# Routing flags laid out with pairs of token blocks innermost

## The chip, the cores and the metric

The kernel runs on one core of a Trainium2 chip. The metric is the device time of one execution in microseconds. The kernel before takes 2205.02 us (median of 3 runs, 2200.27 to 2205.75). The profiled execution took 2211.22 us; its traced span is 2209.5 us.

## The reference, cut to what matters

```python
x = x + xattn(layernorm(x), ctx, ...)        # x: 8 x 512 x 512; 16 heads, 1601 keys
xf = layernorm(x).reshape(-1, 512)           # 4096 tokens
logits = xf @ w_gate                         # 8 experts
top_logits, top_idx = top_k(logits, 2)
weights = softmax(top_logits)
# every token goes through its two experts (512 -> 256 gated -> 512),
# the results are weighted, added, and added to x
```

The kernel does not sort the tokens. It gives each of the 8192 (token, choice) pairs a slot: 72 tiles of 128 lanes, where each tile belongs to one expert. For each slot it needs a list entry: which token sits there, with what weight, and in which slot the token's other choice sits. The change is in the making of that list.

## The kernel before, in words

The program has phases, with a barrier of all engines between them (`phase`, line 35). Attention takes the first 1735 us or so of the span. Then `route` (line 1378) makes the slot list, and `run_experts` (line 1645) gathers the token rows by that list and runs the 72 tiles through the experts.

In `route` the 4096 tokens lie as 128 partitions by TT = 32 blocks. Each choice c (0 or 1) of a token has a tile number (`where`) and a lane in it (`within`). The list is made by matmuls with one-hot flags (lines 1485 to 1490): for each c and each block n, a 128x128 matrix `lane_hot[c][:, :, n]` (token by lane) is the stationary operand, and a 128x432 matrix `marks[c][:, :, :, n]` (token by 6 values x 72 tiles) is the moving one. All 64 products are added up in one bank, `ps_table`, which then holds for each lane and tile the 6 values: row, block, weight high, weight low, other tile, other lane.

Before the change both flag arrays have the block index innermost: `lane_hot` is [128 lanes][32 blocks] and `marks` is [6 values][72 tiles][32 blocks] of 2-byte numbers in each partition. A matmul takes one n, so it reads every 32nd number, one each 64 bytes, in both operands.

VectorE fills them. Its program in this part is: `lane_hot` for both c by a comparison of a constant array `lane` with the broadcast `within` (line 1590); the flags `tile_hot` in the same way from `number` and `where` (line 1592); then for each c five products of 128x2304 (lines 1598 to 1605), of which the last is written over `tile_hot` itself and waits for ScalarE's product of the sixth value (line 1475). TensorE's 32 products for c = 0 wait for `marked[0]`, those for c = 1 for `marked[1]`. The constants `lane` and `number` are made by ScalarE at the start of the phase (lines 1468 and 1469) as full 128x4096 and 128x2304 arrays, which lie in space borrowed from `marks[1]`.

The same phase loads and splits the experts' weights, 8 experts in 3 pieces each. For each piece: a DMA to `e_raw` (waits for the VectorE split of the same piece of the expert before), ScalarE's high part (line 1465), VectorE's low part (`low_pieces`, line 1502). The low parts are written out by hand between VectorE's routing steps. The last before the list are `low_pieces(3)` at line 1614; then VectorE waits for `listed` (line 1616), reads the bank and works out `slots`, `partners`, `targets` (lines 1617 to 1633), and does the three low parts that remain (line 1634). That ends the phase.

Of the kernel before, what the change touches and what calls it, by code (L numbers as in the profile page):

```python
# [7 lines left out]
F16 = mybir.dt.float16  # L8
# [3 lines left out]
ALU = mybir.AluOpType  # L12
ACT = mybir.ActivationFunctionType
AX = mybir.AxisListType

P = 128
# [3 lines left out]
E, TOPK, FF = 8, 2, 256  # L20
# [42 lines left out]
def sbuf(nc, held, name, shape, dt):  # L63
    return held.enter_context(nc.sbuf_tensor(name, shape, dt))


def banks(nc, held, names, dt=F32):
    n = 512 if dt == F32 else 1024
    return [held.enter_context(nc.psum_tensor(x, [P, n], dt)) for x in names]
# [137 lines left out]
TT = B * N // P  # L207
TILES = 72
# [1164 lines left out]
VALUES = 6  # L1373
# [4 lines left out]
def route(nc, k, t):  # L1378

    with ExitStack() as held, phase(nc) as (block, sem):  # L1380
# [5 lines left out]
        def weight_piece(e, n, part):  # L1386
            return t["wi"][:, e, part, 2 * n:2 * n + 2, :] if n < 2 else t["wo"][:, e, part, :, :]

        sb = lambda name, shape, dt=F32: sbuf(nc, held, "r_" + name, shape, dt)
# [9 lines left out]
        pos, where_f, where, within_f, within = (  # L1399
            sb("pos", [P, TOPK, TT]), sb("where_f", [P, TOPK, TT]), sb("where", [P, TOPK, TT], F16),  # L1400
            sb("within_f", [P, TOPK, TT]), sb("within", [P, TOPK, TT], F16))
        w_high = sb("w_high", [P, TOPK, TT], F16)
        w_low = sb("w_low", [P, TOPK, TT], F16)
        block_i, block_f = sb("block_i", [P, TT], I32), sb("block_f", [P, TT], F16)
        row_i, row_1 = sb("row_i", [P, 1], I32), sb("row_1", [P, 1])
        spare = sb("spare", [P, 1])
        lane_i, number_i = sb("lane_i", [P, P, 1], I32), sb("number_i", [P, TILES, 1], I32)
        lane_hot = [sb(f"lane_hot{c}", [P, P, TT], F16) for c in range(TOPK)]
        marks = [sb(f"marks{c}", [P, VALUES, TILES, TT], F16) for c in range(TOPK)]
        tile_hot = [marks[c][:, VALUES - 1, :, :] for c in range(TOPK)]  # L1410
        number = marks[1][:, 2, :, :]
        lane = marks[1][:, 0:2, :, :].rearrange("p v q n -> p (v q n)")[:, 0:P * TT].rearrange("p (l n) -> p l n", n=TT)
        second, tile_1, other_tile, other_lane = (
            sb("second", [P, TOPK, TT]), sb("tile_1", [P, TOPK, TT]), sb("other_tile", [P, TOPK, TT], F16),
            sb("other_lane", [P, TOPK, TT], F16))
# [12 lines left out]
        ps_before, ps_total, ps_table = banks(nc, held, ["r_pb", "r_pt", "r_ps"])  # L1428
        made, spread, step, hot_ready, summed, gap_ready, ratio_ready, tile_ready, listed = (
            sem("r_" + n) for n in ("made", "spread", "step", "hot_ready", "summed", "gap_ready", "ratio_ready",  # L1430
                                    "tile_ready", "listed"))
        marked = [sem(f"r_marked{c}") for c in range(TOPK)]

        @block.gpsimd
        def _(pool):
            pool.iota(experts_i[:, :], [[1, E]], base=0, channel_multiplier=0)
            pool.iota(tile_i[:, :], [[1, TILES]], base=0, channel_multiplier=0)
            pool.iota(lane_i[:, :, :], [[1, P]], base=0, channel_multiplier=0)
            pool.iota(number_i[:, :, :], [[1, TILES]], base=0, channel_multiplier=0)
            pool.iota(block_i[:, :], [[1, TT]], base=0, channel_multiplier=0)  # L1440
            pool.iota(row_i[:, :], [[1, 1]], base=1, channel_multiplier=1)
            pool.affine_select(out=before[:, :], in_=k["ones"][:, :], compare_op=ALU.is_gt, fill=0.0, base=0,
                               pattern=[[1, P]], channel_multiplier=-1).then_inc(made, 1)
# [15 lines left out]
        @block.scalar  # L1459
        def _(act):  # L1460
            def high_pieces(experts):
                for e in experts:
                    for n in range(PIECES):
                        act.wait_ge(loaded[n], 32 * (e + 1))
                        act.mul(weight_piece(e, n, 0), raw[n][:, :, :], WSCALE).then_inc(high, 1)

            act.wait_ge(made, 1)
            act.copy(lane, lane_i[:, :, :].to_broadcast([P, P, TT]))
            act.copy(number, number_i[:, :, :].to_broadcast([P, TILES, TT])).then_inc(spread, 1)
            act.wait_ge(gap_ready, 1)  # L1470
            act.activation(ratio[:, :], gap[:, :], ACT.Exp, scale=1.0 / WSCALE).then_inc(ratio_ready, 1)
            high_pieces(range(0, 4))
            for c in range(TOPK):
                act.wait_ge(tile_ready, TOPK)
                act.activation(marks[c][:, 0, :, :], tile_hot[c], ACT.Identity,
                               scale=row_1[:, 0:1]).then_inc(marked[c], 1)
                high_pieces(range(4 + 2 * c, 6 + 2 * c))

        @block.tensor
        def _(pe):  # L1480
            pe.wait_ge(hot_ready, 1)
            flat = any_hot_b[:, :, :].rearrange("p t e -> p (t e)")
            pe.matmul(ps_before[:, 0:TT * E], before_b[:, :], flat, start=True, stop=True)
            pe.matmul(ps_total[:, 0:TT * E], ones_b[:, :], flat, start=True, stop=True).then_inc(summed, 1)
            for c in range(TOPK):
                pe.wait_ge(marked[c], 2)
                for n in range(TT):
                    last = pe.matmul(ps_table[:, 0:VALUES * TILES], lane_hot[c][:, :, n],
                                     marks[c][:, :, :, n].rearrange("p v q -> p (v q)"),
                                     start=(c == 0 and n == 0), stop=(c == TOPK - 1 and n == TT - 1))  # L1490
            last.then_inc(listed, 1)

        @block.vector
        def _(dve):
# [3 lines left out]
            def low_pieces(count):  # L1498
                flat = lambda a: a.rearrange("p a b -> p (a b)")
                for e, n in itertools.islice(pieces, count):  # L1500
                    dve.wait_ge(high, PIECES * e + n + 1)
                    dve.scalar_tensor_tensor(out=flat(weight_piece(e, n, 1)), in0=flat(raw[n][:, :, :]),
                                             scalar=WSCALE, in1=flat(weight_piece(e, n, 0)), op0=ALU.mult,
                                             op1=ALU.subtract).then_inc(split, 1)

            for n in range(TT):
                last = dve.max(best[:, n, :], t["logits"][:, n, :])
            done(last)
            for n in range(TT):
                last = dve.max_index(index[:, n, :], best[:, n, :], t["logits"][:, n, :])  # L1510
# [8 lines left out]
            for c in range(TOPK):  # L1519
                last = dve.tensor_tensor(hot[:, c, :, :], experts[:, None, :].to_broadcast([P, TT, E]),  # L1520
                                         chosen[:, c, :, None].to_broadcast([P, TT, E]), ALU.is_equal)
# [33 lines left out]
            for c in range(TOPK):  # L1555
                last = dve.tensor_tensor(hot[:, c, :, :], hot[:, c, :, :], place[:, :, :], ALU.mult)
# [26 lines left out]
            for c in range(TOPK):  # L1583
                dve.tensor_tensor(other_tile[:, c, :], tile_1[:, 1 - c, :], second[:, c, :], ALU.mult)
                last = dve.tensor_tensor(other_lane[:, c, :], within_f[:, 1 - c, :], second[:, c, :], ALU.mult)
            done(last)

            dve.wait_ge(spread, 1)
            for c in range(TOPK):
                dve.tensor_tensor(lane_hot[c][:, :, :], lane, within[:, c, None, :].to_broadcast([P, P, TT]), ALU.is_equal)  # L1590
            for c in range(TOPK):
                dve.tensor_tensor(tile_hot[c], number, where[:, c, None, :].to_broadcast([P, TILES, TT]),
                                  ALU.is_equal).then_inc(tile_ready, 1)
            dve.wait_ge(tile_ready, TOPK)
            low_pieces(1)
            for c in range(TOPK):
                over = lambda a: a[:, c, None, :].to_broadcast([P, TILES, TT])
                dve.tensor_tensor(marks[c][:, 1, :, :], tile_hot[c],
                                  block_f[:, None, :].to_broadcast([P, TILES, TT]), ALU.mult)
                dve.tensor_tensor(marks[c][:, 2, :, :], tile_hot[c], over(w_high), ALU.mult)  # L1600
                low_pieces(2)
                dve.tensor_tensor(marks[c][:, 3, :, :], tile_hot[c], over(w_low), ALU.mult)
                dve.tensor_tensor(marks[c][:, 4, :, :], tile_hot[c], over(other_tile), ALU.mult)
                dve.wait_ge(marked[c], 1)
                dve.tensor_tensor(tile_hot[c], tile_hot[c], over(other_lane), ALU.mult).then_inc(marked[c], 1)
                low_pieces(2)


# [238 lines left out]
def program(nc, x, ctx_t, wq, bq, wkv_t, bkv, wp, bp, w_gate, wi_0, wi_1, w_out, out):  # L1847
# [14 lines left out]
    with ExitStack() as held:  # L1862
# [52 lines left out]
        t["slots"], t["partners"], t["targets"] = (sb(n, [P, TILES], U32) for n in ("slots", "partners", "targets"))  # L1915
        t["slot_weight"] = sb("slot_weight", [P, TILES])
        route(nc, k, t)
        run_experts(nc, k, t)

# [22 lines left out]
```

## Time and profile before

| | |
|---|---|
| median of 3 runs | 2205.02 us |
| profiled execution, time | 2211.22 us |
| its span | 2209.5 us |
| TensorE busy | 84% of the span |
| VectorE busy | 81% |
| ScalarE busy | 61% |
| GpSimd busy | 44% |

The shares are means over phases with different limits. The routing phase is some 110 us of the span, and it is read by its own timeline: for each engine, when an instruction starts, how long it takes, and what ended the idle time before it. PEclk is the clock that TensorE was granted, as a share of 2.4 GHz; 0.50 is 1.2 GHz.

### The profile page before, as it was taken

How to read it: one execution, taken by the hardware profiler on the slowest of the kernel's cores; microseconds unless marked ns; L12 is line 12 of the kernel's file. 1: busy time of each engine (PE TensorE's matmuls, PEld its weight loads, DVE VectorE, ACT ScalarE, POOL GpSimd, SP SyncE). 2: the span in 40 equal slices, each digit the busy share in tenths (PEclk: the TensorE clock that was granted, in tenths of full speed). 3: DMA queues.
4: the chain of work that ended last, by engine and by line, in shares of the span. 5: the costliest groups of instructions: out<-in, count | busy, mean ns of one | idle time of the engine just before them, and what ended most of it. 6: DMA issues, size and time to landing. Idle time of an engine off the chain costs nothing. (4 is left out here: it accounts for less than half of the span.)

```text
span 2209.5 us, 60580 instructions
## 1 busy us (share of the span) xinstructions
PE 1849.1 (84%) x24745; PEld 1264.9 (57%) x24804; DVE 1795.7 (81%) x2402; ACT 1351.7 (61%) x1944; POOL 969.0 (44%) x900
## 2 busy tenths in 40 slices
PE   1379998999988989998989898989986147999996
PEld 1247676666666666666666666667763012555553
DVE  4469999899998998998999999988996582666665
ACT  0347877777777777777777787777766431233222
POOL 0011653383265336434723553373435101677675
PEclk9889999999999999999999999999998556999998
DMA  2322332233233223323322331331221351566785
GB/s 86 99 80 56 96 93 53 78 103 85 59 99 101 61 74 100 95 56 87 108 79 62 105 105 44 88 108 56 65 54 49 99 159 62 176 200 218 242 264 176
DMA packets 152822, 225.40 MB, mean 102 GB/s; under 512 B 33860, under 2 KB 87108, under 8 KB 152544
## 3 DMA queue, kind: packets, MB, share of 16 engines
q1 hardware_dynamic: 130736, 166.89, 26.2%
q0 software_dynamic: 21808, 54.58, 8.0%
q8 instruction: 202, 3.31, 0.7%
q14 instruction: 76, 0.62, 0.1%
HBM read 131.37 MB, written 71.32 MB: 92 GB/s over the span
## 5 line engine op out<-in xcount | busy, mean ns | idle before, releaser
L764 DVE TENSOR_TENSOR a_p_low<-a_p 128x1024 f16<-128x1024 f32 (+1 forms) x896 | 1095.5, 1245 | 141.5 <-ACT a_p L642 133.6
L642 ACT ACTIVATE a_p<-ps_s 128x1024 f32<-128x1024 f32 (+1 forms) x896 | 862.6, 967 | 390.4 <-PE ps_s L493 382.1
L493 PE MATMUL ps_s<-a_q_stack,a_k_stack 96*128 96x512 f16 (+1 forms) x1664 | 516.0, 385 | 81.1 <-DMA a_k_stack<-a_k_parts 55.0
L604 PE MATMUL ps_o<-a_v,a_p 128*128 128x65 f16 (+1 forms) x6656 | 448.3, 195 | 19.3 <-ACT a_o_sums L668 8.9
L604 PE MATMUL ps_o<-a_v,a_p_low 128*128 128x65 f16 (+1 forms) x6656 | 448.0, 194 | 0.0
L526 PEld LDWEIGHTS ps_p<-wkv,a_ctx 128*128 128x128 f16 x4992 | 329.6, 99 | 166.1 <-DVE a_v L779 59.0
L526 PE MATMUL ps_p<-wkv,a_ctx 128*128 128x128 f16 x4992 | 378.7, 221 | 44.4 <-DVE a_v L779 44.1
L604 PEld LDWEIGHTS ps_o<-a_v,a_p 128*128 128x128 bf16 (+1 forms) x6656 | 352.7, 99 | 101.2 <-DVE a_p_low L764 26.9
L510 PE MATMUL ps_p<-a_ctx,wkv 128*128 128x384 f16 (+2 forms) x1536 | 347.6, 336 | 36.9 <-DVE a_ctx L402 34.2
L604 PEld LDWEIGHTS ps_o<-a_v,a_p_low 128*128 128x128 f16 (+1 forms) x6656 | 318.4, 98 | 0.0
L510 PEld LDWEIGHTS ps_p<-a_ctx,wkv 128*128 128x128 f16 x1536 | 147.7, 98 | 184.6 <-DVE a_ctx L402 30.9
L905 POOL TENSOR_TENSOR a_o_full<-a_o_sums 128x128 f32<-128x128 f32 x128 | 133.4, 1071 | 214.9 <-ACT a_o_sums L668 214.9
L402 POOL TENSOR_TENSOR a_ctx<-a_ctx_raw,a_ctx 128x384 f16<-128x384 f32 (+2 forms) x112 | 169.0, 1521 | 116.1 <-ACT a_ctx L678 115.2
L1735 PE MATMUL f_ph<-wi_parts,f_xt 128*128 x864 | 200.8, 383 | 2.6 <-DVE f_xt L1802 2.6
L909 POOL TENSOR_TENSOR a_o_full<-a_o_full,o_inv 128x128 f32<-128x128 f32 x128 | 142.0, 1138 | 84.8 <-DVE o_inv L786 84.1
L493 PEld LDWEIGHTS ps_s<-a_q_stack,a_k_stack 96*128 96x128 f16 (+1 forms) x1664 | 114.4, 100 | 87.2 <-issue 81.7
L1676 POOL DMA_INDIRECT f_xs<-d_xr,slots x72 | 82.2, 1142 | 181.2 <-POOLq L48 109.4
L956 POOL TENSOR_TENSOR a_o_full<-a_o_full,a_x_in 128x512 f32<-128x512 f32 x32 | 87.7, 2741 | 153.7 <-DVE a_o_full L865 153.7
L1735 PEld LDWEIGHTS f_ph<-wi_parts,f_xt 128*128 128x128 f16 x864 | 84.8, 98 | 106.0 <-issue 6.0
L1788 ACT ACTIVATE f_gate<-f_ph 128x256 f32<-128x256 f32 x72 | 27.7, 385 | 142.6 <-PE f_ph L1735 142.6
L950 POOL TENSOR_TENSOR a_x_in<-a_x_in,bp_row 128x512 f32<-128x512 f32 x32 | 55.3, 1730 | 125.5 <-DMA a_x_in<-in_x_dram 125.4
L936 POOL TENSOR_SCALAR a_q_nmean<-a_q_mv 128x4 f32<-128x4 f32 x8 | 5.7, 719 | 234.3 <-DVE a_q_rstd L791 234.3
(232 smaller groups left out, 2211.9 us busy)
## 6 DMA issues: line engine op xcount, KB each, us to landing
a_k_stack<-a_k_parts SPq DMA_DIRECT2D x384, 80.0 KB, 2.1
d_ys<-f_y SPq DMA_DIRECT2D x72, 256.0 KB
a_ctx_raw<-in_ctx_dram SPq DMA_DIRECT2D x64, 192.0 KB, 2.5
a_q_stack<-d_q_t SPq DMA_DIRECT2D x96, 128.0 KB, 3.6
a_xm<-in_x_dram SPq DMA_DIRECT2D x8, 1024.0 KB, 5.9
a_ctx_raw<-in_ctx_dram SPq DMA_DIRECT2D x32, 256.0 KB, 4.6
d_q_t<-a_q_parts SPq DMA_DIRECT2D x32, 256.0 KB, 2.7
d_q_full<-a_xm SPq DMA_DIRECT2D x32, 256.0 KB, 2.9
```

The lines of the kernel that those rows point to most:

```text
L402: eng.tensor_tensor(t["ctx"][:, 1, c, a:e], t["ctx_raw"][p % NRAW][:, 0:e - a], t["ctx"][:, 0, c, a:e], ALU.subtract).then_inc(ctx_split, 1)
L493: mm = pe.matmul(t["ps_s"][s % 2][0:r, n * N:(n + 1) * N], t["k_stack"][v % 2][0:TERMS * DH, j, kt * P:kt * P + r], t["q_stack"][v % 2][0: ...
L510: mm = pe.matmul(bank(job)[:, 0:e - a], t["wkv"][:, w_part, c, c0:c0 + P], t["ctx"][:, x_part, c, a:e], start=(m == 0), stop=(m == TERMS * ...
L526: mm = pe.matmul(bank(job)[:, n * P:(n + 1) * P], t["ctx"][:, x_part, c, kt * P:(kt + 1) * P], t["wkv"][:, w_part, c, c0:c0 + P], start=(m ...
L604: mm = pe.matmul(t["ps_o"][:, q * VC:(q + 1) * VC], part[0:r, n * N + q * P:n * N + (q + 1) * P], val, start=(g == 0 and n == 0 and low == ...
L642: act.activation(t["p"][s % NP][0:r, 0:len(tiles) * N], t["ps_s"][s % 2][0:r, 0:len(tiles) * N], ACT.Exp, scale=float(DH) ** -0.5 / WSCALE ...
L764: dve.tensor_tensor(t["p_low"][s % NP][0:r, 0:n], full, high, ALU.subtract).then_inc(lows, 1)
L905: last = pool.tensor_tensor(heads[:, j], sums[:, j, :, 0:DH], sums[:, j, :, DH:2 * DH], ALU.add)
L909: last = pool.tensor_tensor(heads[:, j], heads[:, j], t["o_inv"][:, v, j, :, None].to_broadcast([P, QT, DH]), ALU.mult)
L956: pool.tensor_tensor(t["o_full"][b % 2][:, m, :], t["o_full"][b % 2][:, m, :], t["x_in"][i % 2][:, :], ALU.add).then_inc(x2_ready, 1)
L1676: pool.indirect_dma_start(out=xs[n % NX][:, :], out_offset=None, in_=t["xr"][:, :], in_offset=bass.IndirectOffsetOnAxis(ap=t["slots"][:, n ...
L1735: last = pe.matmul(ps_h[n % 2][:, :], xt[n % 2][:, x_part, c, :], t["wi"][:, bass.ds(e, 1), w_part, c, :].rearrange("p a f -> p (a f)"), s ...
```

## The change

The block index n is split into n // 2 and n % 2. The arrays become `lane_hot` [16][128 lanes][2] and `marks` [16][6 values][72 tiles][2]. A matmul for one n now reads every second number, one each 4 bytes, in both operands, in a run of 128 or 432. The matmuls are the same in number, order and shape. `lane` and `number` become small arrays of their own (128x2 and 72x2 numbers), read again for each of the 16 outer steps. VectorE's twelve products and comparisons of 2304 elements and two of 4096 keep their element counts; the per-token operand is now read as a pair that is repeated for all lanes or tiles (`over`), where before a run of 32 was repeated.

No instruction moves. In ScalarE's program, at the start of the routing phase, the two casts that make the constants become smaller:

```order
 L1459 UNCONDITIONAL_BRANCH
 L1468 ACT_TABLE_LOAD
-L1468 CAST r_marks<-r_lane_i 128x4096
-L1469 CAST r_marks<-r_number_i 128x2304
+L1468 CAST r_lane<-r_lane_i 128x256
+L1469 CAST r_number<-r_number_i 128x144
 L1471 ACTIVATE r_ratio<-r_gap 128x32
 L1465 ACTIVATE wi_parts<-e_raw 128x1024 x2
```

Nothing else stands there than before; the shapes are what changed.

```diff
-        lane_hot = [sb(f"lane_hot{c}", [P, P, TT], F16) for c in range(TOPK)]
-        marks = [sb(f"marks{c}", [P, VALUES, TILES, TT], F16) for c in range(TOPK)]
-        tile_hot = [marks[c][:, VALUES - 1, :, :] for c in range(TOPK)]
-        number = marks[1][:, 2, :, :]
-        lane = marks[1][:, 0:2, :, :].rearrange("p v q n -> p (v q n)")[:, 0:P * TT].rearrange("p (l n) -> p l n", n=TT)
+        lane, number = sb("lane", [P, P, 2], F16), sb("number", [P, TILES, 2], F16)
+        lane_hot = [sb(f"lane_hot{c}", [P, TT // 2, P, 2], F16) for c in range(TOPK)]
+        marks = [sb(f"marks{c}", [P, TT // 2, VALUES, TILES, 2], F16) for c in range(TOPK)]
+        mark = lambda c, v: marks[c][:, :, v, :, :]
+        tile_hot = [mark(c, VALUES - 1) for c in range(TOPK)]
...
-            act.copy(lane, lane_i[:, :, :].to_broadcast([P, P, TT]))
-            act.copy(number, number_i[:, :, :].to_broadcast([P, TILES, TT])).then_inc(spread, 1)
+            act.copy(lane[:, :, :], lane_i[:, :, :].to_broadcast([P, P, 2]))
+            act.copy(number[:, :, :], number_i[:, :, :].to_broadcast([P, TILES, 2])).then_inc(spread, 1)
...
-                    last = pe.matmul(ps_table[:, 0:VALUES * TILES], lane_hot[c][:, :, n],
-                                     marks[c][:, :, :, n].rearrange("p v q -> p (v q)"),
+                    last = pe.matmul(ps_table[:, 0:VALUES * TILES], lane_hot[c][:, n // 2, :, n % 2],
+                                     marks[c][:, n // 2, :, :, n % 2].rearrange("p v q -> p (v q)"),
...
+            def over(a, count):
+                return a.rearrange("p (h two) -> p h two", two=2)[:, :, None, :].to_broadcast([P, TT // 2, count, 2])
+
+            def along(a, count):
+                return a[:, None, :, :].to_broadcast([P, TT // 2, count, 2])
+
             dve.wait_ge(spread, 1)
             for c in range(TOPK):
-                dve.tensor_tensor(lane_hot[c][:, :, :], lane, within[:, c, None, :].to_broadcast([P, P, TT]), ALU.is_equal)
+                dve.tensor_tensor(lane_hot[c][:, :, :, :], along(lane, P), over(within[:, c, :], P), ALU.is_equal)
...
-                dve.tensor_tensor(marks[c][:, 2, :, :], tile_hot[c], over(w_high), ALU.mult)
+                dve.tensor_tensor(mark(c, 2), tile_hot[c], over(w_high[:, c, :], TILES), ALU.mult)
...
```

The other products of `marks` and ScalarE's (line 1475) are rewritten in the same way as the last pair of lines.

## Rows read from the trace of the kernel before

**Rows 1.** The page: span, and the granted TensorE clock in 40 slices (tenths).
```profile
span 2209.5 us, 60580 instructions
...
PEclk9889999999999999999999999999998556999998
```

**Rows 2.** Waits, 1735 to 1870 us: total us, times, longest us.
```profile
POOL f_xs L1676 <- POOLq L48: 109.4, 1, 109.4
...
DVE r_table L1617 <- PE r_ps L1488: 24.2, 1, 24.2
...
DVE r_marks L1605 <- ACT r_marks L1475: 2.9, 1, 2.9
```

**Rows 3.** Line 1488's instructions: ns min/median/max, first and last start.
```profile
L1488 PEld LDWEIGHTS r_ps<-r_marks,r_lane_hot x64: 141/148/162, 1795.7 to 1841.3; 128*128 128x128 f16 x64
L1488 PE MATMUL r_ps<-r_marks,r_lane_hot x64: 900/916/939, 1795.7 to 1842.1; 128*128 128x432 f16 x64
```

**Rows 4.** Windows: length, busy us (count) of PE, PEld, DVE, ACT, POOL; PEclk, DMA.
```profile
1795.60:1843.00 47.40, 47.29 (x64) 9.41 (x64) 18.62 (x19) 12.59 (x11) 0.00 (x0) 0.50 0.34 101
```

**Rows 5.** Timeline of TensorE: start us, us, line, operation, [idle before, releaser].
```profile
1795.68 47.29 PE L1488 MATMUL r_ps<-r_marks,r_lane_hot 128*128 128x432 f16 x64 [39.45 <-DVE r_marks L1605]
1856.82 1.03 PE L1724 MATMUL f_px<-id,f_xs 128*128 128x128 f16 x8 [13.85 <-DMA f_xs<-d_xr,slots]
1858.73 5.30 PE L1735 MATMUL f_ph<-wi_parts,f_xt 128*128 x12 [0.88 <-DVE f_xt L1802]
...
1865.40 2.76 PE L1735 MATMUL f_ph<-wi_parts,f_xt 128*128 x12 [0.87 <-DVE f_xt L1802]
```

**Rows 6.** Windows at the start of the experts: the granted clock rises.
```profile
1863.00:1864.00 1.00, 1.00 (x5) 0.45 (x4) 0.00 (x0) 0.00 (x0) 0.00 (x0) 0.50 0.57 234
1864.00:1865.00 1.00, 0.53 (x9) 0.36 (x6) 0.43 (x1) 0.38 (x1) 0.00 (x0) 0.99 0.02 8
```

**Rows 7.** Timeline of VectorE, around its wait for the list.
```profile
1808.13 1.36 DVE L1605 TENSOR_TENSOR r_marks<-r_marks,r_other_lane 128x2304 f16<-128x2304 f16 x1 [2.89 <-ACT r_marks L1475]
...
1817.53 1.22 DVE L1502 SCALAR_TENSOR_TENSOR wo_parts<-e_raw,wo_parts 128x1024 f16<-128x1024 f32 x1 [1.14 <-ACT wo_parts L1465]
1843.00 0.61 DVE L1617 COPY r_table<-r_ps 128x432 f32<-128x432 f32 x1 [24.25 <-PE r_ps L1488]
...
1846.08 2.36 DVE L1502 SCALAR_TENSOR_TENSOR wi_parts<-e_raw,wi_parts 128x1024 f16<-128x1024 f32 x2
1848.36 1.22 DVE L1502 SCALAR_TENSOR_TENSOR wo_parts<-e_raw,wo_parts 128x1024 f16<-128x1024 f32 x1
```

**Rows 8.** Timeline of ScalarE: constants, exponential, and the last expert's high parts.
```profile
1742.73 3.60 ACT L1468 CAST r_marks<-r_lane_i 128x4096 f16<-128x4096 int32 x1
...
1753.50 0.23 ACT L1471 ACTIVATE r_ratio<-r_gap 128x32 f32<-128x32 f32 x1 [5.16 <-DVE r_gap L1512]
...
1818.83 1.06 ACT L1465 ACTIVATE wi_parts<-e_raw 128x1024 f16<-128x1024 f32 x1 [1.33 <-DMA e_raw<-in_L_ffn_wi_dram]
1821.30 1.06 ACT L1465 ACTIVATE wi_parts<-e_raw 128x1024 f16<-128x1024 f32 x1 [1.42 <-DMA e_raw<-in_L_ffn_wi_dram]
1823.09 1.06 ACT L1465 ACTIVATE wo_parts<-e_raw 128x1024 f16<-128x1024 f32 x1 [0.73 <-DMA e_raw<-in_L_ffn_wo_dram]
```

**Rows 9.** Groups of VectorE instructions by shape: count | busy us, mean ns | idle.
```profile
L1590 DVE TENSOR_TENSOR r_lane_hot<-r_marks,r_within 128x4096 f16<-128x4096 f16 x2 | 4.5, 2288 | 0.0
...
L1598 DVE TENSOR_TENSOR r_marks<-r_marks,r_block_f 128x2304 f16<-128x2304 f16 x2 | 2.7, 1352 | 0.0
...
L1520 DVE TENSOR_TENSOR r_hot<-r_experts,r_chosen 128x256 f32<-128x256 f32 x2 | 0.8, 422 | 0.0
...
L1609 DVE TENSOR_TENSOR r_passed<-r_tile_f,r_starts 1x576 f32<-1x576 f32 x1 | 0.7, 740 | 0.0
...
L1523 DVE TENSOR_TENSOR r_any_hot<-r_hot 128x256 f32<-128x256 f32 x1 | 0.4, 425 | 0.0
```

**Rows 10.** Timeline of GpSimd: its first gather for the experts.
```profile
1851.97 1.19 POOL L1676 DMA_INDIRECT f_xs<-d_xr,slots  x1 [109.42 <-POOLq L48]
```

More of the change, by code:

```diff
@@ L1474, in _ @@
                 act.wait_ge(tile_ready, TOPK)
-                act.activation(marks[c][:, 0, :, :], tile_hot[c], ACT.Identity,
+                act.activation(mark(c, 0), tile_hot[c], ACT.Identity,
                                scale=row_1[:, 0:1]).then_inc(marked[c], 1)
@@ L1586, in _ @@
             done(last)
+            def over(a, count):
+                return a.rearrange("p (h two) -> p h two", two=2)[:, :, None, :].to_broadcast([P, TT // 2, count, 2])
+            def along(a, count):
+                return a[:, None, :, :].to_broadcast([P, TT // 2, count, 2])
             dve.wait_ge(spread, 1)
             for c in range(TOPK):
-                dve.tensor_tensor(lane_hot[c][:, :, :], lane, within[:, c, None, :].to_broadcast([P, P, TT]), ALU.is_equal)
+                dve.tensor_tensor(lane_hot[c][:, :, :, :], along(lane, P), over(within[:, c, :], P), ALU.is_equal)
             for c in range(TOPK):
-                dve.tensor_tensor(tile_hot[c], number, where[:, c, None, :].to_broadcast([P, TILES, TT]),
+                dve.tensor_tensor(tile_hot[c], along(number, TILES), over(where[:, c, :], TILES),
                                   ALU.is_equal).then_inc(tile_ready, 1)
@@ L1596, in _ @@
             for c in range(TOPK):
-                over = lambda a: a[:, c, None, :].to_broadcast([P, TILES, TT])
-                dve.tensor_tensor(marks[c][:, 1, :, :], tile_hot[c],
-                                  block_f[:, None, :].to_broadcast([P, TILES, TT]), ALU.mult)
-                dve.tensor_tensor(marks[c][:, 2, :, :], tile_hot[c], over(w_high), ALU.mult)
+                dve.tensor_tensor(mark(c, 1), tile_hot[c], over(block_f[:, :], TILES), ALU.mult)
+                dve.tensor_tensor(mark(c, 2), tile_hot[c], over(w_high[:, c, :], TILES), ALU.mult)
                 low_pieces(2)
-                dve.tensor_tensor(marks[c][:, 3, :, :], tile_hot[c], over(w_low), ALU.mult)
-                dve.tensor_tensor(marks[c][:, 4, :, :], tile_hot[c], over(other_tile), ALU.mult)
+                dve.tensor_tensor(mark(c, 3), tile_hot[c], over(w_low[:, c, :], TILES), ALU.mult)
+                dve.tensor_tensor(mark(c, 4), tile_hot[c], over(other_tile[:, c, :], TILES), ALU.mult)
                 dve.wait_ge(marked[c], 1)
-                dve.tensor_tensor(tile_hot[c], tile_hot[c], over(other_lane), ALU.mult).then_inc(marked[c], 1)
+                dve.tensor_tensor(tile_hot[c], tile_hot[c], over(other_lane[:, c, :], TILES),
+                                  ALU.mult).then_inc(marked[c], 1)
                 low_pieces(2)
```

## The prediction, made before the changed kernel ran

> **What bounds the kernel now.** I read the page first. TensorE's clock is at 0.9 or more in most of the 40 slices and dips to 0.5 in two of them after slice 30 [rows 1]; slices are 55 us long, so these two lie about the routing phase, between attention and experts. The shares of busy time say nothing there. The waits of that stretch come next. The longest is GpSimd's, 109.4 us until the barrier [rows 2]: the experts start when the routing phase ends, with nothing of the experts beside it. So what the routing phase loses or gains at its end goes into the span one to one, and the question is what ends that phase.
>
> VectorE ends it: its last instruction is the third of the last low parts, from 1848.36 to 1849.58 [rows 7]. Before these it worked off the list, from 1843.00 to 1846.08, and before the list it stood idle for 24.25 us until TensorE had finished line 1488 [rows 2, 7]. TensorE runs its 64 products without a pause from 1795.68 to 1842.97 [rows 5], though it had to wait for nothing: the marks of the second choice were ready when VectorE's last product ended at 1808.13 + 1.36 = 1809.49 [rows 7]. So between 1818.75 (VectorE's last low part before the wait ends, 1817.53 + 1.22) and 1843.00 the phase is bound by the rate of TensorE alone, and the reader should ask what that rate is.
>
> It is 47.29 us / 64 = 0.739 us for one product of 432 columns, or 1.71 ns per column. The granted clock is 0.50 all through, 1.2 GHz [rows 4]. At that same clock the experts' first 12 products of 512 columns took 5.30 us [rows 5, 6], 0.442 us each, 0.863 ns per column. They read their operands in one run; line 1488 reads a number each 64 bytes. The flag products thus take twice as long per column as dense ones at an equal clock. The record of 916 ns for one matmul [rows 3] is longer than the 739 from start to start, since they overlap; I use starts.
>
> **The change part by part.** *Moving operand.* Now a number each 4 bytes. I take the dense rate: 432 x 0.863 = 0.373 us per product at 1.2 GHz. At 2.4 GHz the experts' next 12 took 2.76 us, 0.230 us each for 512 columns, so 0.194 us for 432 [rows 5, 6]. The ends for the unknown stride of 4 bytes are the dense rate and today's 0.739 us (no gain at all); 4 bytes is nearest to the dense rows of 2-byte steps, so I take these. *Stationary operand.* 148 ns per load now [rows 3]; between nothing and 148 ns shows: if the load were not hidden behind the product before, a product would take 0.373 + 0.148 = 0.52 us. In the dense rows a load stands for each product as well, and 0.442 us for 512 columns leaves 0.015 us for it over 512 / 1.2 GHz = 0.427, so I take it as hidden.
>
> *The first 32 products* start at 1795.7 as before and need at most 32 x 0.373 = 11.9 us, to 1807.6. That is before 1809.49, so they no longer queue in front of the second 32. *The second 32* start at 1809.5 and take 32 x 0.194 = 6.2 us if the clock is up, 32 x 0.373 = 11.9 us if it isn't: end at 1815.7 to 1821.4. Which one is open: the clock rose in the experts within 7.1 us of TensorE's first work (1856.82 to about 1863.9 [rows 5, 6]), while in 47 us of line 1488 it never did [rows 4]. With dense reads I would expect it to rise in the first batch; whether it survives the pause of some 2 to 4 us before the second I can't tell.
>
> *VectorE until the list.* Two comparisons of 4096 elements at 2.288 us and twelve of 2304 at 1.352 us [rows 9]. From these two, 1792 elements are 0.936 us, 0.522 ns per element or 1.04 ns per pair: the numbers are taken in pairs. After the change outputs are still dense runs (144 or 4096 numbers), the first input too, and the second is one pair read again and again. I take no change. The ends are below nothing only by noise, since the element rate can't rise, and above by the unpaired rate (the first rival below). The row nearest to a repeated word is line 1520, where the second input repeats one 4-byte number 8 times: 422 ns for 256, against 425 with plain operands [rows 9]. So re-reading a word costs nothing there.
>
> *ScalarE.* The cast of 3.60 us [rows 8] and its smaller neighbour shrink to a small part. ScalarE then waits 5.16 us for VectorE's gap anyway [rows 8], so the saving is worth nothing. Its two products of 2304 keep count and runs: nothing. *Memory, DMA.* The loads of weights follow VectorE's splits, which don't move before the list.
>
> *What is late next.* VectorE's own three low parts before the wait end at 1818.75. With a warm TensorE (1815.7) the list starts at about 1818.8, and ends 3.08 us later (1843.00 to 1846.08 [rows 7]) at 1821.9. Then the last expert's low parts, 1.14 us from start to start, each no sooner than ScalarE's high part: these end at 1819.9, 1822.4 and 1824.15 [rows 8]. So the last starts at 1824.2 and ends at 1825.4, where the weights' DMA and ScalarE are the limit. Against 1849.58 that is 24.2 us. With a cold TensorE the list starts at 1821.5, ends at 1824.6, and three low parts (3.50 us, 1846.08 to 1849.58) end at 1828.1: 21.5 us. So whether the clock is up is worth only 2.7 us. The 24.25 us of wait vanish, but up to 2.7 us come back as the wait for the last piece's load.
>
> *The experts* start as before, after the same barrier, 12 us or more after TensorE's last flag product, and I take their cold first tile as it is. If the clock were up there, 5.30 - 2.76 = 2.5 us would be gained besides.
>
> The sum: between 21.5 and 24.2 us, and I take 23. The profiled execution would go from 2211.22 to 2188 us, its span to 2186.5. It lies 6.2 us above the median of the runs; the same saving on the median gives 2205.0 - 23 = 2182 us, own range 2177 to 2187 (26.7 us of gain at most, 21.5 at least, and some 3 us of spread between runs).
>
> **The rivals.** *A. VectorE loses its pairs, or pays for the repeated one.* Its rate in unpaired rows is (740 - 425) / 320 = 0.984 ns per element (lines 1609 and 1523 [rows 9]). 4096 elements would take 0.740 + 3520 x 0.984 = 4.20 us (+1.92), 2304 would take 2.44 us (+1.09): 2 x 1.92 + 12 x 1.09 = 16.9 us. The 2.9 us wait for ScalarE [rows 2] may swallow some of it, so 14.0 to 16.9. VectorE reaches its wait at 1832.8 to 1835.7, TensorE ends at 1829.7 to 1838.3; 6.6 us later the phase ends, at 1839.4 to 1844.9. The gain shrinks to 5 to 10 us: 2198 us. Against it stand line 1520's 422 ns; for it, that no row shows a 2-byte pair repeated. The Trainium skill has a rule on this side, in DVE Microarchitecture Reference, section 5.2: a port streams at full rate only over runs of at least two adjacent 4-byte words, and single words cost about 0.65 cycle more; line 1520 does not agree for words that are repeated. By that rule as an estimate (0.68 ns for each of 17920 pairs) 12.2 us would be added, and the time would be about 2193 us. Its section 5.1 says that two elements still run packed, which no run here shows yet.
>
> *B. A step of 4 bytes still costs TensorE something,* or the weight loads show: 0.52 us per product. The first 32 (16.6 us) end at 1812.3, after 1809.5, so the second 32 start there and end at 1829.0; 6.6 us later, at 1835.6, the phase ends: gain 14 us, 2191 us. For it: the loads are also strided. Against: step and load come to little in the dense rows.
>
> *C. Slower.* VectorE reads the pairs unpacked and pays for each jump back as TensorE does for its stride (1.71 - 0.863 = 0.85 ns): 2 x 0.984 + 0.85 = 2.82 ns per pair instead of 1.04, times 17920 pairs = 31.9 us more. The list would wait for VectorE, not TensorE. The point from which this decides is 24.3 us more on VectorE (1818.75 to 1843.00), or 2.4 ns per pair. At 31.9 us the phase is 7.6 us longer, less up to 2.9: about 2211 us.
>
> *D. The change doesn't do what it says:* TensorE's 0.739 us comes from something other than the stride, and stays. Then 2205 us. Against: dense products at the same clock, 15 us later, take half per column.
>
> **How the numbers follow.** Forecast 0.80; A 0.09; B 0.05; C 0.03; D 0.03. A measurement of this kernel tells about 0.3%, 6.6 us, from no change, so faster means below 2198.4. Faster: 0.80 + 0.05 + a bit over half of A = 0.90. Same: the rest of A and most of D, 0.06. Slower: C and a remainder, 0.04. The range from 2176 to 2192 holds the forecast's own range and B, about 0.82; A's 2198 is left out.
>
> **What would show it.** Line 1488 in two batches, 32 products in 6 to 12 us each, with a pause until about 1809.5; VectorE's line 1617 starting near 1819 to 1821.5, with a wait of under 3 us before it; the twelve products at 1.35 us and two comparisons at 2.29 us; then a short wait of VectorE for ScalarE's last high part; GpSimd's first gather at about 1829 instead of 1851.97 [rows 10]; the experts of equal length. The prediction is wrong if the twelve products take 2.4 us, if TensorE's starts stay over 0.5 us apart, or if the experts take longer by what the phase saved.

## The result, and the profile after

The changed kernel takes 2187.34 us (median of 7 runs, 2181.22 to 2191.30) against 2210.30 us of the kernel before in the same comparison (7 runs). The medians lie 22.96 us apart. The ratio of the two sets of runs is 0.9887, 95% interval 0.9864 to 0.9910: by it the gain is 25.0 us (19.9 to 30.1). Forecast were 2182 us, a gain of 23 us and a range of 2176 to 2192. The profiled execution took 2184.58 us, its span 2182.8 us, 26.7 us less than before.

Where did the 26.7 us go? The first row of the judging step that ends attention (line 1021) starts at 1736.42 us, 3.02 us earlier than before (1739.44): that is attention, which the change doesn't touch, and in a second profile of the changed kernel (e10) the same row starts at 1738.01. From that row to GpSimd's first gather it was 112.53 us, now it is 87.79: 24.74 us less. From the gather to the end it was 357.5 us and is 358.6: 1.1 us more. So the phase between line 1021 and the gather carries the gain, and I use its length as the measure in all that follows.

The timeline of TensorE after the change (start us, us, what, idle time before and its releaser), to be held against [rows 5] and [rows 10]:

```profile
1736.42 0.19 PE L1021 MATMUL j_ps<-ones,j_fit 128*1 128x1 f32 x2 [7.14 <-DVE j_fit L1014]
...
1791.90 7.61 PE L1488 MATMUL r_ps<-r_marks,r_lane_hot 128*128 128x432 f16 x32 [38.99 <-DVE r_marks L1609]
1805.80 9.09 PE L1488 MATMUL r_ps<-r_marks,r_lane_hot 128*128 128x432 f16 x32 [6.30 <-DVE r_marks L1609]
1828.98 1.03 PE L1729 MATMUL f_px<-id,f_xs 128*128 128x128 f16 x8 [14.09 <-DMA f_xs<-d_xr,slots]
1830.89 5.13 PE L1740 MATMUL f_ph<-wi_parts,f_xt 128*128 x12 [0.88 <-DVE f_xt L1807]
```

```profile
1824.21 1.19 POOL L1681 DMA_INDIRECT f_xs<-d_xr,slots  x1 [84.68 <-POOLq L48]
```

One train of 47.29 us has become two batches of 7.61 and 9.09 us, with a pause of 6.30 us in which TensorE waits for the second choice's marks. Before, that pause was hidden in the backlog.

The same stretch of VectorE (answers to [rows 7]):

```profile
1804.39 1.36 DVE L1609 TENSOR_TENSOR r_marks<-r_marks,r_other_lane 128x2304 f16<-128x2304 f16 x1 [2.93 <-ACT r_marks L1475]
...
1813.74 1.23 DVE L1502 SCALAR_TENSOR_TENSOR wo_parts<-e_raw,wo_parts 128x1024 f16<-128x1024 f32 x1 [0.86 <-ACT wo_parts L1465]
1814.93 0.61 DVE L1622 COPY r_table<-r_ps 128x432 f32<-128x432 f32 x1
...
1818.01 2.36 DVE L1502 SCALAR_TENSOR_TENSOR wi_parts<-e_raw,wi_parts 128x1024 f16<-128x1024 f32 x2
1820.59 1.22 DVE L1502 SCALAR_TENSOR_TENSOR wo_parts<-e_raw,wo_parts 128x1024 f16<-128x1024 f32 x1 [0.23 <-ACT wo_parts L1465]
```

The wait of 24.25 us for the list is gone: line 1622 follows the low part before it at once. It is a near thing: TensorE's last product ends at 1805.80 + 9.09 = 1814.89, and line 1622 starts at 1814.93. What VectorE waits for now is ScalarE (2.93, 0.86, 0.23 us). Its own work has not changed, by shape (answers to [rows 9]; mean ns in the last part but one):

```profile
L1596 DVE TENSOR_TENSOR r_lane_hot<-r_lane,r_within 128x4096 f16<-128x4096 f16 x2 | 4.5, 2287 | 0.0
...
L1603 DVE TENSOR_TENSOR r_marks<-r_marks,r_block_f 128x2304 f16<-128x2304 f16 x2 | 2.7, 1352 | 0.0
```

And line 1488's instructions (ns min/median/max), to be held against [rows 3]:

```profile
L1488 PEld LDWEIGHTS r_ps<-r_marks,r_lane_hot x64: 96/97/145, 1791.9 to 1814.3; 128*128 128x128 f16 x64
L1488 PE MATMUL r_ps<-r_marks,r_lane_hot x64: 350/352/562, 1791.9 to 1814.5; 128*128 128x432 f16 x64
```

Windows over the two batches and the pause (length, busy us of PE, PEld, DVE, ACT, POOL, then the granted clock):

```profile
1792.00:1795.00 3.00, 3.00 (x10) 1.18 (x10) 3.00 (x3) 1.06 (x1) 0.00 (x0) 0.54 0.27 69
1795.00:1799.50 4.50, 4.50 (x24) 2.09 (x22) 4.50 (x5) 2.02 (x2) 0.00 (x0) 1.00 0.71 219
...
1802.00:1804.00 2.00, 0.00 (x0) 0.00 (x0) 0.00 (x0) 2.00 (x2) 0.00 (x0) 0.50 0.40 140
1806.00:1810.00 4.00, 4.00 (x12) 1.58 (x11) 3.90 (x7) 0.00 (x0) 0.00 (x0) 0.50 0.49 136
1812.00:1814.90 2.90, 2.89 (x16) 1.26 (x13) 2.04 (x2) 1.06 (x1) 0.00 (x0) 1.00 0.73 221
```

The granted clock goes up to 2.4 GHz within the first batch, falls to 1.2 GHz in the pause, and rises again within the second. So the second batch is mostly cold, which here means at 1.2 GHz: 9.09 us.

### The profile page after: what moved, and what is told of

The parts are those of the page before. It is cut to its first block and busy times, and to the rows that moved or that the text cites. A ratio compares the mean times of both kernels' runs of the same rounds, so it can differ in the third digit from the quotient of the medians.

```text
span 2182.8 us, 60639 instructions
## 1 busy us (share of the span) xinstructions
PE 1822.8 (84%) x24804; PEld 1263.3 (58%) x24804; DVE 1795.8 (82%) x2402; ACT 1346.1 (62%) x1944; POOL 970.5 (44%) x900
## 5 line engine op out<-in xcount | busy, mean ns | idle before, releaser
L905 POOL TENSOR_TENSOR a_o_full<-a_o_sums 128x128 f32<-128x128 f32 x128 | 147.8, 1183 | 202.6 <-ACT a_o_sums L668 202.6
L909 POOL TENSOR_TENSOR a_o_full<-a_o_full,o_inv 128x128 f32<-128x128 f32 x128 | 129.6, 1041 | 84.6 <-DVE o_inv L786 83.9
```

The lines of the kernel that those rows point to most:

```text
L905: last = pool.tensor_tensor(heads[:, j], sums[:, j, :, 0:DH], sums[:, j, :, DH:2 * DH], ALU.add)
L909: last = pool.tensor_tensor(heads[:, j], heads[:, j], t["o_inv"][:, v, j, :, None].to_broadcast([P, QT, DH]), ALU.mult)
```

## The experiments

They ran in three sets, each with the kernel before beside them, which took 2249 us (e1 to e4), about 2262 us (e5 to e8) and 2211 us (e9, e10). In e1, 395 us lie between the gather and the end, in e8 406 us, against 358.6 us above and 356.6 us in e10: there, in the experts' phase, nearly all of the difference between the sets lies. Its cause was not looked for. Ratios to the kernel before in the same set, and the length of the phase from line 1021 to the first gather, can be compared. The phase is read from one profile each; e5, e6 and e7 ran only once, for their profile, and have no ratio.

| | phase, us | 64 flag products | wait for the list, us | ratio to before |
|---|---|---|---|---|
| before | 112.53 | 47.29 | 24.25 | |
| changed | 87.79 | 7.61 + 9.09 | 0 | 0.9887 |
| e1 marks only | 86.92 | 8.49 + 8.41 | 0 | 0.9892 (0.9860 to 0.9923) |
| e2 lanes only | 111.80 | 46.52 | 23.40 | 1.0003 (0.9982 to 1.0024) |
| e3 no pair | 104.28 | 7.63 + 7.33 | 0 | 0.9972 (0.9954 to 0.9991) |
| e4 ScalarE first | 83.89 | 7.88 + 7.58 | 0 | 0.9881 (0.9858 to 0.9905) |
| e5 step 8 bytes | 89.44 | 12.40 + 12.41 | 3.37 | |
| e6 step 16 bytes | 112.60 | 48.88 | 25.93 | |
| e7 step 32 bytes | 113.64 | 49.80 | 26.86 | |
| e8 no pause | 87.86 | 8.05 + 6.27 | 0 | 0.9884 (0.9837 to 0.9932) |
| e9 GpSimd | 90.10 | 7.69 + 8.61 | 1.49 | 0.9905 (0.9882 to 0.9929) |
| e10 changed again | 87.02 | 8.69 + 8.60 | 0 | 0.9903 (0.9881 to 0.9926) |

**e1: only the marks in pairs**

```diff
+        WL, WM = 32, 2
...
-        lane_hot = [sb(f"lane_hot{c}", [P, TT // 2, P, 2], F16) for c in range(TOPK)]
...
+        lane_hot = [sb(f"lane_hot{c}", [P, TT // WL, P, WL], F16) for c in range(TOPK)]
```

WL and WM are the numbers of blocks that lie innermost in `lane_hot` and in `marks`; the other uses of the two arrays follow them, here and in e2, e3, e5, e6 and e7.

> The marks (moving operand) in pairs as in the changed kernel, lane_hot (stationary) in the old layout with a 64-byte step; one VectorE wait after the lane comparisons is added, under 0.1 us. Theory: the moving operand's step alone set the rate. Then the 64 flag products go at 0.36 us (1.2 GHz) and 0.18 us (2.4 GHz) from start to start as in the changed kernel, though the weight loads stay at about 148 ns, since these are hidden behind the product before; VectorE's wait for the list is under 1 us and the time is the changed kernel's within 2 us. Rival 1: the stationary operand's step costs as much: products at 0.6 us or more, and a wait of 8 us or more for the list. Rival 2: the loads show only where the clock is up: 0.23 instead of 0.18 us, the batches some 1.5 us longer.

The whole gain is there with the marks alone: the phase is 86.92 us, the list is not waited for. The theory held but for a trace of rival 2. The weight loads of lane_hot stay at 148 ns. There is one load for each product, so their starts give the rate too: where the clock is up 19 loads follow each other in 3.75 us, (3.75 - 0.15) / 18 = 0.200 us each. In e8, with paired lanes, 34 go in 6.39 us, (6.39 - 0.10) / 33 = 0.191 us:

```profile
1805.76 3.75 PEld L1490 LDWEIGHTS r_ps<-r_marks,r_lane_hot 128*128 128x128 f16 x19 [0.20 <-issue]
```

```profile
1810.89 6.39 PEld L1493 LDWEIGHTS r_pw<-r_marks,r_lane_hot 128*128 128x128 f16 x34
```

**e2: only the lanes in pairs**

```diff
+        WL, WM = 2, 32
...
-        marks = [sb(f"marks{c}", [P, TT // 2, VALUES, TILES, 2], F16) for c in range(TOPK)]
...
+        marks = [sb(f"marks{c}", [P, TT // WM, VALUES, TILES, WM], F16) for c in range(TOPK)]
```

> lane_hot (stationary operand) in pairs, the marks (moving operand) in the old layout with a 64-byte step. Theory: nothing is gained: weight loads fall from 148 to about 97 ns, the products stay at 0.739 us from start to start, in one train of 47.3 us, at a granted clock of 0.50, and the time is that of the kernel before within 2 us. Rival: the stationary step has a part in it: 0.65 us or less per product, so 5 us or more gained.

Nothing in the time (1.0003), as the theory said:

```profile
1792.31 46.52 PE L1489 MATMUL r_ps<-r_marks,r_lane_hot 128*128 128x432 f16 x64 [38.92 <-DVE r_marks L1612]
```

0.727 instead of 0.739 us per product: the stationary operand's step was worth 0.8 us of the 47, the moving one's the rest. The weight loads fell from 148 to 124 ns (median) and not to 97: the 97 ns were read in the changed kernel, where most of them ran at the upper clock, and here the granted clock is 0.50 all through.

**e3: the block index wholly outermost, without the pair**

```diff
-        lane, number = sb("lane", [P, P, 2], F16), sb("number", [P, TILES, 2], F16)
...
+        WL, WM = 1, 1
+        lane, number = sb("lane", [P, P, WL], F16), sb("number", [P, TILES, WM], F16)
```

and the same in both flag arrays and in `over` and `along`.

> The whole block index outermost, no pair: TensorE reads both operands in dense runs (2-byte step), VectorE's per-token operand becomes one number repeated along the row. Theory (the pair is there for VectorE; this is the rival A of the prediction made real): the two comparisons of 4096 take 4.2 us and the twelve operations of 2304 take 2.4 us, 14 to 17 us more on VectorE before the list; TensorE's products at 0.36 or 0.18 us as in the changed kernel, so 4 bytes cost nothing against 2; the time is 14 to 17 us above the changed kernel, about 2200 us. Rival: VectorE keeps the pair rate (2.29 and 1.35 us) with a repeated single number: the changed kernel's time within 2 us.

```profile
L1599 DVE TENSOR_TENSOR r_lane_hot<-r_lane,r_within 128x4096 f16<-128x4096 f16 x2 | 8.8, 4422 | 0.0
...
L1606 DVE TENSOR_TENSOR r_marks<-r_marks,r_block_f 128x2304 f16<-128x2304 f16 x2 | 5.1, 2551 | 0.0
```

The theory held. VectorE's operations take 4.42 and 2.55 us instead of 2.29 and 1.35, and the phase is 16.5 us longer than in the changed kernel. TensorE gained almost nothing by fully dense runs: at the upper clock 24 loads, one for each product, start in 4.40 us, (4.40 - 0.10) / 23 = 0.187 us each, against 0.191 with 4 bytes. So the pair is what VectorE needs and what TensorE hardly notices.

```profile
1835.04 4.40 PEld L1489 LDWEIGHTS r_ps<-r_marks,r_lane_hot 128*128 128x128 f16 x24 [0.21 <-issue]
```

**e4: ScalarE's second product ahead of the high parts**

```diff
+            act.wait_ge(tile_ready, TOPK)
             for c in range(TOPK):
-                act.wait_ge(tile_ready, TOPK)
                 act.activation(mark(c, 0), tile_hot[c], ACT.Identity,
                                scale=row_1[:, 0:1]).then_inc(marked[c], 1)
-                high_pieces(range(4 + 2 * c, 6 + 2 * c))
+            high_pieces(range(4, 8))
```

> The changed kernel, with ScalarE's second product of the marks (line 1475, c = 1) put ahead of the high parts of experts 4 and 5 in its program. Theory: what bounds the end of the phase is now VectorE's own program, so its 2.93 us wait for that product goes and the last flag product and the last low part come 2 to 3 us earlier, the span 2 to 3 us shorter. Rival: the weights' load chain bounds it (each piece's load waits for the low part of the expert before), so the 2.9 us come back as waits for high parts of experts 5 to 7 and the phase ends less than 1 us earlier.

The phase is 83.89 us, 3.9 us less than in the changed kernel's first profile and 3.1 less than in e10. From the first lane comparison to the gather, which leaves out what varies ahead of it, it is 46.46 us against 49.27 (changed) and 49.17 (e10): 2.7 to 2.8 us. That is the wait of 2.93 us for ScalarE, nearly whole; the waits for high parts are 0.46, 0.77 and 0.75 us instead of 0.64, 0.86 and 0.23, so only some 0.3 us come back. The theory held. In the time alone e4 can't be told from the changed kernel: 0.9881 against 0.9887 and 0.9903, with intervals of 0.002 to either side. By the trace it is the shortest of all.

**e5, e6, e7: the step of the moving operand**

```diff
+        WL, WM = 2, 4
...
-        marks = [sb(f"marks{c}", [P, TT // 2, VALUES, TILES, 2], F16) for c in range(TOPK)]
...
+        marks = [sb(f"marks{c}", [P, TT // WM, VALUES, TILES, WM], F16) for c in range(TOPK)]
```

This is e5; in e6 WM is 8 and in e7 16, so 4, 8 and 16 blocks lie innermost; VectorE's operations kept their 1.35 us in all three.

> As the changed kernel, but the marks with 4 blocks innermost: the moving operand is read at an 8-byte step. Theory: the cost of a step begins only where each number lies in another 16-byte line; two numbers share a line here, so the products keep 0.36 us at 1.2 GHz and 0.18 us at 2.4 GHz from start to start. Rival: the cost grows with the step from 4 bytes on: 0.4 us or more at 1.2 GHz.

> The marks with 8 blocks innermost: a 16-byte step of the moving operand. Theory: every number lies in another 16-byte line, so the full cost is there, 0.74 us from start to start as with 64 bytes, at a granted clock that stays at 0.50, and VectorE waits some 24 us for the list. Rival: cost grows with the step, so 0.45 to 0.6 us here.

> The marks with 16 blocks innermost: a 32-byte step of the moving operand. Theory: as with 16 and 64 bytes, 0.74 us from start to start. Rival: the cost grows with the step, between the 16-byte result and 0.74 us.

```profile
1791.05 12.40 PE L1489 MATMUL r_ps<-r_marks,r_lane_hot 128*128 128x432 f16 x32 [39.24 <-DVE r_marks L1612]
1804.96 12.41 PE L1489 MATMUL r_ps<-r_marks,r_lane_hot 128*128 128x432 f16 x32 [1.50 <-DVE r_marks L1612]
```

```profile
1791.00:1795.00 4.00, 3.95 (x11) 1.38 (x12) 4.00 (x4) 1.06 (x1) 0.00 (x0) 0.50 0.42 133
1799.00:1803.00 4.00, 4.00 (x12) 1.17 (x10) 1.61 (x2) 2.66 (x2) 0.00 (x0) 1.00 0.63 210
1805.00:1807.00 2.00, 2.00 (x6) 0.65 (x7) 2.00 (x2) 0.00 (x0) 0.00 (x0) 0.98 0.00 0
1807.00:1810.00 3.00, 3.00 (x10) 0.96 (x8) 2.90 (x6) 0.54 (x1) 0.00 (x0) 0.50 0.88 276
```

```profile
1789.29 48.88 PE L1489 MATMUL r_ps<-r_marks,r_lane_hot 128*128 128x432 f16 x64 [38.97 <-DVE r_marks L1612]
```

Both theory and rival of e5 missed; the theories of e6 and e7, full cost and a clock at 0.50, held. The two timeline rows and the four windows are of e5 (8 bytes), the last row is of e6 (16 bytes). With 8 bytes a product takes 0.383 us from start to start, and it does so at 1.2 and at 2.4 GHz alike: the first two windows show 11 and 12 products in 4 us at either clock. So at this step the rate does not follow the granted clock. Per product, from start to start:

| step, bytes | at 1.2 GHz, us | at 2.4 GHz, us |
|---|---|---|
| 2 (e3) | 0.36 | 0.187 |
| 4 (changed, e8) | 0.36 | 0.191 |
| 8 (e5) | 0.383 | 0.383 |
| 16 (e6) | 0.761 | the clock never rose |
| 32 (e7) | 0.775 | the clock never rose |
| 64 (e2) | 0.724 | the clock never rose |
| 64 in both operands (before) | 0.736 | the clock never rose |

The last four are read from the starts of the weight loads; the 0.739 and 0.727 us above are the length of the whole train divided by 64, which holds the end of the last product too.

16 bytes cost twice what 8 do (1.76 and 0.89 ns per number), and beyond 16 the cost stays within some 5%. This fits a cost of about 1.77 ns for each 16 bytes of SBUF that are touched, however many numbers are taken from them: two from each give 0.383, four would give 0.191, which is what 4 bytes show at the upper clock, just above the dense 0.187. It is an explanation that fits and no more: it leaves open why 64 bytes cost a little less than 32. That the 4-byte step lies so near to this limit was not in my prediction. The Trainium skill, in SBUF — State Buffer, Specifications (TRN2), gives SBUF lines of 16 bytes and asks for at least two hits per line for full bandwidth. The trace agrees on the 16 bytes. Two hits nearly do at 1.2 GHz (0.383 us against 0.36) and give half the rate at 2.4 GHz (0.383 against 0.187), where four give nearly the full one (0.191); three were not tried.

**e8: no pause between the batches**

```diff
+                if c == 0:
+                    for _ in range(34):
+                        pe.matmul(ps_warm[:, 0:VALUES * TILES], lane_hot[0][:, 0, :, 0],
+                                  marks[0][:, 0, :, :, 0].rearrange("p v q -> p (v q)"), start=True, stop=True)
```

> The changed kernel with 34 products of the first block's flags into a bank of their own (never read) between the two batches, so that TensorE does not pause. Theory: the granted clock stays at 1.00 from some point in the first batch on, the second batch takes 32 x 0.18 = 5.8 us instead of 9.09, and nothing is gained in time, since VectorE reaches its wait for the list only at the same time as now (its own low parts before it): the time within 2 us of the changed kernel. Rival: the second batch is what the list waits for, and the phase ends 2 us or more earlier; or the clock falls nonetheless, and the batch stays at 9 to 11.5 us.

The theory held, but for 5.8 us, which came out as 6.27. The clock stayed at 1.00 and the second batch was 2.8 us shorter than in the changed kernel; the phase is 87.86 against 87.79 and 87.02 us. The list is read 1.14 us after the start of the low part before it, which is the usual distance between two instructions there (1.19 us in the changed kernel, 1.15 in e10): VectorE's own program is what it waits for. So a warm second batch gains 0.05 us at the most against the changed kernel, and what the clock does between the batches costs next to nothing as long as it rises within the second.

```profile
1825.04 1.23 DVE L1506 SCALAR_TENSOR_TENSOR wo_parts<-e_raw,wo_parts 128x1024 f16<-128x1024 f32 x1 [1.03 <-ACT wo_parts L1465]
1826.18 0.60 DVE L1626 COPY r_table<-r_ps 128x432 f32<-128x432 f32 x1
```

**e9: a third of the low parts on GpSimd**

```diff
+            for e in range(E):
+                pool.wait_ge(high, PIECES * e + 3)
+                pool.tensor_tensor(whole(weight_piece(e, 2, 1)), whole(raw[2][:, :, :]),
+                                   whole(weight_piece(e, 2, 0)), ALU.subtract).then_inc(split[2], 1)
...
                         if n == 2:
+                            act.mul(raw[2][:, :, :], raw[2][:, :, :], WSCALE).then_inc(scaled, 1)
+                            act.wait_ge(scaled, e + 1)
+                            act.copy(weight_piece(e, n, 0), raw[n][:, :, :]).then_inc(high, 1)
...
+                    if n == pool_takes:
+                        continue
```

> The kernel of e4, with the low part of each expert's third piece (8 of the 24) moved from VectorE to GpSimd, which is idle in this phase; ScalarE scales that piece in place first (8 more activations of 1.06 us), since GpSimd then needs only a subtraction. Theory: VectorE's own program bounds the phase, so 8 x 1.14 = 9.1 us less of it makes the phase 6 to 9 us shorter than e4's, counted from the end of attention to the first gather, and VectorE waits little. Rival: the third piece's chain (load about 4 us, 2.1 us ScalarE, 2 to 3 us GpSimd, 8 times in a row: 65 to 75 us) or ScalarE's added work takes over, or VectorE's operations slow down beside GpSimd: under 3 us gained, with VectorE waiting for high parts or TensorE for the marks.

The theory fell and the rival held. The phase is 90.10 us, 6.2 us longer than in e4, though VectorE had 8 low parts less; in the time alone e9 (0.9905) can't be told from e10 (0.9903). Two things show. The one of VectorE and GpSimd that begins second is held up. The low part at 1785.30 takes 3.12 us instead of 1.22 and ends 1.1 us after the subtraction that began at 1785.21 (1787.33), line 1628 at 1808.64 takes 2.67 us instead of 0.74 and ends 0.6 us after the one from 1808.27 (1810.71), and a copy of 8 numbers at 1757.26 takes 1.31 us instead of 0.17. The f16 product at 1799.36 keeps its 1.34 us, but it had begun before the subtraction at 1799.75, and now that one is late: 2.95 us instead of 2.12. A large f16 product that begins while a subtraction runs is not in this trace, so it doesn't show whether the types of the numbers matter. Not everything is held up: between 1756.5 and 1757.2 two copies from PSUM keep their 0.42 and 0.41 us. And the third piece's chain ends last: its final subtraction ends at 1826.58, after VectorE's last work (1821.10 + 2.36 = 1823.46), and the gather follows 2.6 us later.

```profile
1757.26 1.31 DVE L1549 COPY r_sum_b<-r_sum_a 128x8 f32<-128x8 f32 x1
...
1785.30 3.12 DVE L1516 SCALAR_TENSOR_TENSOR wi_parts<-e_raw,wi_parts 128x1024 f16<-128x1024 f32 x1
...
1799.36 1.34 DVE L1618 TENSOR_TENSOR r_marks<-r_marks,r_w_high 128x2304 f16<-128x2304 f16 x1
...
1808.64 2.67 DVE L1628 TENSOR_TENSOR r_passed<-r_tile_f,r_starts 1x576 f32<-1x576 f32 x1
```

```profile
1756.13 2.41 POOL L1448 TENSOR_TENSOR wo_parts<-e_raw,wo_parts 128x1024 f16<-128x1024 f32 x1 [13.93 <-ACT wo_parts L1474]
...
1785.21 2.12 POOL L1448 TENSOR_TENSOR wo_parts<-e_raw,wo_parts 128x1024 f16<-128x1024 f32 x1 [10.44 <-ACT wo_parts L1474]
1799.75 2.95 POOL L1448 TENSOR_TENSOR wo_parts<-e_raw,wo_parts 128x1024 f16<-128x1024 f32 x1 [12.42 <-ACT wo_parts L1474]
1808.27 2.44 POOL L1448 TENSOR_TENSOR wo_parts<-e_raw,wo_parts 128x1024 f16<-128x1024 f32 x1 [5.58 <-ACT wo_parts L1474]
...
1824.46 2.12 POOL L1448 TENSOR_TENSOR wo_parts<-e_raw,wo_parts 128x1024 f16<-128x1024 f32 x1 [5.65 <-ACT wo_parts L1474]
1829.20 1.19 POOL L1695 DMA_INDIRECT f_xs<-d_xr,slots  x1 [2.62 <-POOLq L48]
```

In all, seven VectorE operations are longer than the same ones in e10, by 11.5 us together, which is more than the 8 x 1.14 = 9.1 us that were taken off VectorE. The chain's end adds 1826.58 - 1823.46 = 3.1 us behind VectorE's. These are readings of one trace; no run has one of the two without the other.

**e10: the changed kernel once more**

> The changed kernel once more, on the chip of e9, for a direct comparison. Both theories: ratio to the kernel before 0.988 to 0.990, its phase from the first lane comparison to the first gather 49.3 us.

0.9903, at the upper end of what was expected, and 49.17 us (1775.86 to 1825.03).

## Why the prediction was right

- **What bounds the phase.** TensorE's rate on line 1488, and behind it VectorE's wait: shown by the wait of 24.25 us that went to nothing in the changed kernel and came back as 23.40 us in e2, where the marks alone lie as before.
- **The rate of the products.** Forecast 0.373 us cold (at 1.2 GHz) and 0.194 warm (at 2.4 GHz), measured 0.36 and 0.191. The cold figure was a little high because it divides the whole 5.30 us by 12, the end of the last product with it. The starts of the same products' loads, in the two rows of the kernel before below, lie (1862.97 - 1859.13) / 9 = 0.427 us apart, which makes 0.36 us for 432 columns; so the 0.015 us that the prediction left for a load are not the load's. The experts' dense products were a good stand-in for a step of 4 bytes, and at the upper clock this was in part luck: the prediction took them because 4 bytes are nearest to 2, and e5 shows that at 8 bytes they would have been wrong by a factor of two.

```profile
1859.13 0.15 PEld L1735 LDWEIGHTS f_ph<-wi_parts,f_xt 128*128 128x128 f16 x1 [0.28 <-issue]
...
1862.97 0.15 PEld L1735 LDWEIGHTS f_ph<-wi_parts,f_xt 128*128 128x128 f16 x1 [0.28 <-issue]
```

- **The stationary operand.** Taken as hidden: its step is worth 0.009 us per product in e1 where the clock is up, and 0.012 in e2: at most 0.6 and 0.8 us over all 64.
- **VectorE's operations.** Forecast unchanged, measured 2.287 and 1.352 us. Re-reading a pair costs nothing, and the 12.2 us that the prediction worked out for single words did not come. Rival A was the real risk: e3 makes it happen without the pair, at 4.42 and 2.55 us (the estimate was 4.20 and 2.44) and 16.5 us in the phase (14.0 to 16.9). Rivals B, C and D are ruled out by the rows above.
- **The clock.** Forecast to rise in the first batch, which it did. The pause was taken as 2 to 4 us and was 6.3, since the first batch took 7.61 us and not 11.9; the clock fell in it. I had priced this question at up to 2.7 us. It cost nothing, since even the mostly cold second batch ended (1814.89) where VectorE's own low part did (1814.97), and e8 with a warm batch ends no sooner. That the two ends met was luck: the clock rose within the second batch, and one wholly at 1.2 GHz (an estimate: 32 x 0.36 = 11.5 us) would have ended 2.4 us later.
- **The end of the phase.** The forecast with the list at once after VectorE's low parts was 1818.75 for its start and 1825.4 for the last low part's end. VectorE's first lane comparison now starts 3.77 us earlier (1774.94 against 1778.71), so 1815.0 and 1821.6; measured 1814.93 and 1821.81. From that comparison to the gather the gain is 73.26 - 49.27 = 23.99 us, near the upper of the forecast's two ends (24.2). The prediction's wait for ScalarE's last high part is there, with 0.23 us.
- **The total.** 23 us were taken as the middle of the two clocks, 24.0 are shown from the first lane comparison to the gather, and the interval of the timed runs, 19.9 to 30.1 us, holds both. The kernel before came out at 2210 us in the larger set of runs instead of 2205, so the absolute time lies 5 us higher than forecast (2187.34 against 2182) with nearly the same gain. It is 0.34 us above the forecast's own range of 2177 to 2187 and inside the stated one.

## What to carry to other kernels

Where TensorE reads with a step, compare microseconds per column with a dense product at the same granted clock, by start to start: a factor of two there is a layout and not a clock. The writer and the reader of an array may want different innermost indices, and a pair of 2-byte numbers innermost can serve both: VectorE keeps its pairs, TensorE has four numbers in each 16 bytes. And before offering work to the idle engine, look in a trace at which of its neighbour's operations it holds up, and at the longest chain it becomes part of.

## What the runs showed of the hardware that was not expected

- At a step of 8 bytes the moving operand is read at 0.383 us per 432 columns whether the granted clock is 1.2 or 2.4 GHz; at 16, 32 and 64 bytes at 0.761, 0.775 and 0.724 us, all at 1.2 GHz.
- With steps of 16 bytes and more (the kernel before, e2, e6, e7) TensorE was busy for 46 to 50 us without a break at a granted clock of 0.50 throughout, while with steps of 2 to 8 bytes the clock rose within a batch of 8 to 12 us. In e5 (8 bytes) it also fell from 0.98 to 0.50 in the midst of the second batch, with TensorE busy on either side, as the windows at 1805 and 1807 show, and rose again. So a row that shows TensorE as busy doesn't show that the upper clock will be granted. Why it isn't, no run separates.
- VectorE operations that began while a subtraction of 128x1024 ran on GpSimd (2.12 us by itself) were stretched by about the time that was left of it: 0.74 us to 2.67, 1.22 to 3.12, a copy of 8 numbers from 0.17 to 1.31. A subtraction that began 0.39 us after an f16 product on VectorE was itself stretched, to 2.95 us, and the product was not.
